# A sparse graph layer on one core: the last neighbour sums, the long rows and the search for uncovered rows in a new order

## The reference

```python
mask = A != 0
rank = jnp.cumsum(mask, axis=1) - 1
num_nbr = mask.sum(axis=1)
skip = jnp.where(num_nbr > 5, ceil(num_nbr / 2), 1)
keep = mask & ~((rank + 1) % skip[:, None] == 0)
n_keep = keep.sum(axis=1)
svals = jnp.sort(jnp.where(keep[:, :, None], x[None], big), axis=1)
agg = sum(1/3 * svals[row, max(ceil(q * n_keep) - 1, 0)] for q in (0.25, 0.5, 0.75))
agg = 0.5 * where(n_keep > 0, agg, 0) + 0.5 * x
out = agg @ W.T + b + x
```

## Time and profile before

| | |
|---|---|
| median of 3 runs | 160.31 us (160.06 to 160.69) |
| profiled execution, own time | 158.96 us |
| its span, first to last instruction | 157.1 us |
| busy, share of the span | DVE 66%, ACT 70%, PE 63%, POOL 46% |
| chain that ended last | DMA 53%, DVE 22%, PE 8%, issue 6%, POOL 6% |
| mean granted TensorE clock | 0.88 of full |

### The profile page before, as it was taken

One profiled execution on the slowest core, in us unless ns is written; L12 is line 12 of the kernel. 1 busy time (PEld: TensorE's weight loads), 2 busy tenths in 40 slices (PEclk: granted clock), 3 DMA queues, 4 the chain that ended last, 5 costly groups with the idle time before them and its releaser, 6 DMA issues.

```text
span 157.1 us, 2137 instructions
## 1 busy us (share of the span) xinstructions
PE 98.5 (63%) x568; PEld 52.3 (33%) x569; DVE 103.5 (66%) x449; ACT 110.0 (70%) x136; POOL 72.1 (46%) x118
## 2 busy tenths in 40 slices
PE   0009772778159763287765639854457979789892
PEld 0003321334023331123322114422123867658471
DVE  1002268425880649899972789889599989999931
ACT  3099999888888777887977898667779826363020
POOL 6898000000067772277770037776775068731030
PEclk9999999569965999758998555899977999999999
DMA  5999999999999999999999999999981043422002
GB/s 151 426 434 422 430 434 430 430 427 421 417 422 415 409 396 410 416 422 407 394 402 404 427 430 420 406 405 398 397 335 49 0 124 87 121 55 76 0 4 71
DMA packets 9571, 49.99 MB, mean 318 GB/s; under 512 B 1715, under 2 KB 5307, under 8 KB 6230
## 3 DMA queue, kind: packets, MB, share of 16 engines
q1 hardware_dynamic: 7648, 47.71, 74.8%
q0 software_dynamic: 1760, 2.07, 4.4%
q10 hardware_dynamic: 150, 0.07, 0.2%
HBM read 49.61 MB, written 1.71 MB: 327 GB/s over the span
## 4 chain that ended last, share of the span: by engine, by line
DMA 53%; DVE 22%; PE 8%; issue 6%; POOL 6%; ACT 2%; SPq 1%; POOLq 0%; DVEq 0%
DMA adj<-in_adj 49%; POOL gath_b L464 5%; PE ps_w L663 4%; DMA gath_b<-in_table,idx_b 4%; ACT sq L519 2%; DVE quads_a L1340 2%; DVE hot L911 2%; DVE rec L922 1%; DVE quads_b L1030 1%; DVE quads_b L1028 1%; PE ps_out L768 1%; POOL gath_a L464 1%; DVE merged L1028 1%; DVE merged L1030 1%; PE ps_out L775 1%
## 5 line engine op out<-in xcount | busy, mean ns | idle before, releaser
L519 ACT ACTIVATE sq<-adj 128x3328 bf16<-128x3328 int32 x26 | 77.4, 2977 | 21.9 <-DMA adj<-in_adj 21.9
L663 PE MATMUL ps_w<-sq,hot 128*128 128x416 bf16 x208 | 55.4, 420 | 23.0 <-DVE hot L911 23.0
L663 PEld LDWEIGHTS ps_w<-sq,hot 128*128 128x128 bf16 x208 | 19.4, 112 | 46.1 <-DVE hot L911 29.2
L464 POOL DMA_INDIRECT gath_a<-in_table,idx_a x12 | 12.5, 1044 | 48.5 <-DVEq L987 45.7
L464 POOL DMA_INDIRECT gath_b<-in_table,idx_b x24 | 25.4, 1060 | 7.3 <-issue 7.3
L911 DVE SCALAR_TENSOR_TENSOR hot<-slot_code,ps_place,strip_unit 128x256 bf16<-128x256 f32 (+1 forms) x22 | 11.1, 540 | 20.6 <-PE ps_place L641 19.6
L464 POOL DMA_INDIRECT gath_s<-in_table,idx_s x16 | 17.6, 1101 | 11.2 <-DVE idx_s L975 7.0
L911 DVE SCALAR_TENSOR_TENSOR hot<-slot_code,ps_out,strip_unit 128x256 bf16<-128x256 f32 (+1 forms) x22 | 11.1, 538 | 16.9 <-PE ps_out L641 15.2
L634 PE MATMUL ps_place<-level,mpart 64*128 64x2 bf16 x13 | 2.3, 176 | 19.8 <-ACT classes L529 19.8
L922 DVE MAX8 rec<-ps_w 128x8 f32<-128x208 f32 x32 | 9.7, 367 | 0.0
L634 PEld LDWEIGHTS ps_place<-level,mpart 64*128 64x128 bf16 x13 | 1.2, 96 | 24.9 <-issue 14.8
(11 more groups left out here) (276 smaller groups left out, 194.7 us busy)
## 6 DMA issues: line engine op xcount, KB each, us to landing
adj<-in_adj SPq DMA_DIRECT2D x26, 1664.0 KB, 12.6
out<-res SPq DMA_DIRECT2D x6, 192.0 KB, 2.2
xT<-in_xT SPq DMA_DIRECT2D x1, 896.0 KB, 17.8
xT<-in_xT SPq DMA_DIRECT2D x1, 768.0 KB, 15.7
gath_b<-in_table,idx_b POOLq DMA_INDIRECT x24, 6.2
gath_s<-in_table,idx_s POOLq DMA_INDIRECT x16, 4.7
out<-res SPq DMA_DIRECT2D x1, 256.0 KB, 2.3
out<-res SPq DMA_DIRECT2D x2, 128.0 KB, 1.9
```

The costliest lines, as they stand in the source:

```text
L464: nc.gpsimd.indirect_dma_start(slots[:, k, :], None, x_table, bass.IndirectOffsetOnAxis(ap=indices[:, k:k + 1], axis=0), bounds_check=TABL ...
L519: nc.scalar.activation(sq_ring[t % RING][:], adj_ring[t % RING][:], ACT.Square, accum_out=meta[:, t, 0:1]).then_inc(s_sq, 1)
L663: last = nc.tensor.matmul(ps_w[b % 2][h][:, 0:HW], hot[t % 3][:, s, :], sq_ring[t % RING][:, first:first + HW], start=False, stop=end and ...
```

## The change

Five edits, made together:

- The count of uncovered rows moves on VectorE from ahead of block 7's sort to behind `pick_last`; its sum on TensorE moves from ahead of `own_part_last` to behind `listed_part_last`; its cast moves behind the last copy; SP and GpSimd load it after their last transfers.
- The copy of `places` out of PSUM and the two instructions that make `mrec` and `mwords` move from VectorE to ScalarE.
- Block 6's picks are summed on TensorE, by three multiplications of 512 columns each (`turn_alone`); VectorE's two additions for it go. Block 7 gets these two additions instead (in `pick_last`) and is then turned like the other blocks, in two halves, so that `turn_last` with `ident`, `weigh_last` and one ScalarE copy go; VectorE copies the second half.
- The factors of the long rows are made on 16 partitions (`mweigh`), in five columns, spread by one multiplication, and used straight from PSUM.
- The transposes of `mgath` come ahead of `own_part_last`, the two `long_part`s ahead of `turn_last`, and `WARM` goes from 24 to 12.

```diff
@@ SyncE, GpSimd
-            sp.wait_ge(s_sln, 1)
-            n_slow = sp.value_load(slow_n[0:1, 0:1], min_val=0, max_val=N)
             for h in range(2):
...
+            sp.wait_ge(s_sln, 1)
+            n_slow = sp.value_load(slow_n[0:1, 0:1], min_val=0, max_val=N)
...
+            for k in range(2):
+                nc.gpsimd.memset(medge[:, k:k + 1], 15.0 - 2 * k)
+            for k in range(3):
+                nc.gpsimd.memset(msign[:, k:k + 1], 1.0 if k == 1 else -1.0)
@@ ScalarE
             find_spots(6)
+            act.wait_ge(s_hot, NT)
+            for k in range(2):
+                last = nc.scalar.activation(places[:, k:NT:2, :], ps_class[k], ACT.Copy)
+            last.then_inc(s_kept, 1)
             comb_copy(1)
             out_copy(0)
             out_copy(1)
+            act.wait_ge(s_mrec, 1)
+            nc.scalar.activation(mrec[:], ps_mrec, ACT.Copy)
+            nc.scalar.activation(mwords[:], ps_mrec[:, 3:35], ACT.Copy, scale=UNIT).then_inc(s_mcopy, 1)
...
             act.wait_ge(s_combps, NB)
-            nc.scalar.activation(comb[LAST % 2][:, 0:P], ps_comb[:, 0:P], ACT.Copy).then_inc(s_comb, 1)
-            act.wait_ge(s_yps, 1)
-            nc.scalar.activation(y_sb[:], ps_y, ACT.Copy).then_inc(s_y, 1)
+            nc.scalar.activation(comb[LAST % 2][:, 0:2 * P], ps_comb[:, 0:2 * P], ACT.Copy).then_inc(s_comb, 1)
@@ TensorE
+            def turn_alone():
+                pe.wait_ge(s_spots_late, ALONE - 1)
+                pe.wait_ge(s_comb, ALONE)
                 for k, part in enumerate((order[:, 1, :], pick[:, 0, :], pick[:, 1, :])):
                     pe.wait_ge(s_picks, k + 1)
-                    last = nc.tensor.matmul(ps_comb[:, 0:P], part, ident[:], start=(k == 0), stop=(k == 2))
+                    last = nc.tensor.matmul(ps_comb[:], part, late_at(ALONE), start=(k == 0), stop=(k == 2))
                 last.then_inc(s_combps, 1)
-            def weigh_last():
-                pe.wait_ge(s_comb, NB)
-                nc.tensor.matmul(ps_y, comb[LAST % 2][:, 0:P], w_pool[:], start=True, stop=True).then_inc(s_yps, 1)
+            def turn_last():
+                pe.wait_ge(s_spots_late, LAST - 1)
+                pe.wait_ge(s_comb, LAST)
+                pe.wait_ge(s_agg_s, 1)
+                for h, bank in enumerate((ps_comb, ps_w[1][0])):
+                    nc.tensor.matmul(bank[:, 0:2 * P], agg[:, LAST, :], late_spots[:, 3, 2 * h * P:(2 * h + 2) * P],
+                                     start=True, stop=True).then_inc(s_combps, 1)
...
             own_part(6)
+            turn_alone()
             pe.wait_ge(s_mdiag, 1)
-            nc.tensor.matmul(ps_mn, ones_f[0:MID, :], mdiag[:].rearrange("p a m -> p (a m)"), start=True,
-                             stop=True).then_inc(s_mwide, 1)
-            turn(6)
+            nc.tensor.matmul(ps_w[0][1][:, 256:256 + 5 * MID], ones_f[0:MID, :],
+                             mdiag[:].rearrange("p q m -> p (q m)"), start=True, stop=True).then_inc(s_mwide, 1)
             listed_part(6)
-            pe.wait_ge(s_slsum, 1)
-            nc.tensor.matmul(ps_slow, ones_f[:], slow_sum[:], start=True, stop=False)
-            nc.tensor.matmul(ps_slow, ones_f[0:MID, :], mbad[:], start=False, stop=True).then_inc(s_slps, 1)
-            own_part_last()
             pe.wait_ge(s_mgath, 32)
             for u in range(2):
                 last = nc.tensor.transpose(ps_mT[:, u * P:(u + 1) * P], mgath[:, u, :], ident[:])
             last.then_inc(s_mT, 1)
+            own_part_last()
             keep_busy(WARM)
             pe.wait_ge(s_magg, 1)
             nc.tensor.matmul(ps_my, maggT[:], wT[:], start=True, stop=True).then_inc(s_myps, 1)
             keep_busy(WARM_LATE)
+            for h in range(2):
+                long_part(h)
             turn_last()
-            long_part(0)
-            weigh_last()
-            long_part(1)
             listed_part_last()
+            pe.wait_ge(s_slsum, 1)
+            nc.tensor.matmul(ps_slow, ones_f[:], slow_sum[:], start=True, stop=False)
+            nc.tensor.matmul(ps_slow, ones_f[0:MID, :], mbad[:], start=False, stop=True).then_inc(s_slps, 1)
@@ VectorE, pick_last
+                dve.wait_ge(s_combps, ALONE + 1)
...
+                step(v.tensor_tensor(pick[:, 2, :], pick[:, 0, :], T[:, 1, :], ALU.add))
+                v.tensor_tensor(agg[:, LAST, :], pick[:, 2, :], pick[:, 1, :], ALU.add).then_inc(s_agg_s, 1)
+            def copy_comb_half():
+                dve.wait_ge(s_combps, NB + 1)
+                v.tensor_copy(comb[LAST % 2][:, 2 * P:4 * P], ps_w[1][0][:, 0:2 * P]).then_inc(s_comb_late, 1)
@@ VectorE, the factors of the long rows
-            v.tensor_scalar(mdiag[:, 0, :], ident[0:MID, 0:MID], n, None, ALU.mult)
...
-            step(v.tensor_scalar(mdiag[:, 1, :], ident[0:MID, 0:MID], mvalid[:, 1:2], None, ALU.mult))
-            dve.sem_inc(s_mdiag, 1)
+            v.tensor_tensor(mdiag[:], ident[0:MID, 0:MID].unsqueeze(1).broadcast_to([MID, 5, MID]),
+                            mweigh[:, 0:5].unsqueeze(2).broadcast_to([MID, 5, MID]), ALU.mult).then_inc(s_mdiag, 1)
...
+            dve.wait_ge(s_mwide, 1)
+            v.tensor_tensor(mpart[:, :, 0:4].rearrange("p m (s c) -> p s m c", c=2), msort[:, :, :, 4:6],
+                            ps_mn[:, 0:4, :].rearrange("p (s c) m -> p s m c", c=2), ALU.mult)
+            did(v.tensor_tensor(mpart[:, :, 4], msort[:, 1, :, 7], ps_mn[:, 4, :], ALU.mult))
```

More of the change, by code:

```diff
@@ L48 @@
 UNIT = float(1 << ID_BITS)
-WARM = 24
+WARM = 12
 WARM_LATE = 3
@@ L187, in build @@
         mkeys = sb("mkeys", [MID, MID], F32)
-        mdiag = sb("mdiag", [MID, 2, MID], F32)
+        mweigh = sb("mweigh", [MID, 7], F32)
+        mdiag = sb("mdiag", [MID, 5, MID], F32)
         msel = sb("msel", [P, 2, 8], F32)
@@ L500, in _ @@
                 bounds_check=ROWS - 1, oob_is_err=True, compute_op=ALU.add).then_inc(s_scat, 16)
+            pool.wait_ge(s_sln, 1)
+            n_slow = pool.value_load(slow_n[0:1, 0:1], min_val=0, max_val=N)
             with pool.If(n_slow > 0):
@@ L1168, in _ @@
                     merge_quads()
-            for k in range(2):
-                last = v.tensor_copy(places[:, k:NT:2, :], ps_class[k])
-            last.then_inc(s_kept, 1)
             merge_middle()
@@ L1190, in _ @@
             did(v.tensor_tensor(pb[:, :, 0, :], pg[:, :, 0, :], pg[:, :, 1, :], ALU.min))
-            dve.wait_ge(s_mrec, 1)
-            step(v.tensor_copy(mrec[:], ps_mrec))
-            whole = did(v.tensor_scalar(mwords[:], mrec[:, 3:35], UNIT, None, ALU.mult))
+            dve.wait_ge(s_mcopy, 1)
             g1 = did(v.tensor_scalar(mgone[:, 0:1], n, 12.0, 5.0, ALU.is_ge, ALU.add))
@@ L1284, in _ @@
                                          own_slot[:].unsqueeze(1).broadcast_to([P, 2, 8]), ALU.mult))
-            need(summed)
-            v.tensor_tensor(agg[:, ALONE, :], pick[:, 2, :], T[:, 1, :], ALU.add).then_inc(s_agg_s, 1)
             need(chosen)
@@ L1290, in _ @@
             v.tensor_copy(midx[:], midx_f[:]).then_inc(s_midx, 1)
+            dve.wait_ge(s_gath_s[1], KEYS * 16)
+            pg = gath_s[1][:].rearrange("p (a c) d -> p a c d", c=2)
+            low_high(pb[:, :, 0, :], pb[:, :, 1, :], pg[:, :, 0, :], pg[:, :, 1, :])
+            layer_done()
+            low_high(qa[:, :, 0, :], qa[:, :, 1, :], qb[:, :, 0, :], qb[:, :, 1, :])
+            layer_done()
+            low_high(B[:, :, 1, :], B[:, :, 2, :], A[:, :, 1, :], A[:, :, 2, :])
+            layer_done()
+            low_high(S[:, 3:11:7, :], S[:, 1:9:7, :], B[:, 0, 1:3, :], B[:, 1, 1:3, :])
+            low_high(S[:, 11, :], None, A[:, 0, 3, :], A[:, 1, 3, :])
+            low_high(None, S[:, 0, :], A[:, 0, 0, :], A[:, 1, 0, :])
+            layer_done()
+            low_high(S[:, 4:6, :], S[:, 6:8, :], S[:, 10:12, :], S[:, 0:2, :])
+            layer_done()
+            dve.wait_ge(s_mval, 1)
+            for m in range(MID):
+                for sign in range(2):
+                    last = v.max(msort[:, sign, m, :], mval[:, sign, m, :])
+            did(last)
+            layer_done()
+            dve.wait_ge(s_mwide, 1)
+            v.tensor_tensor(mpart[:, :, 0:4].rearrange("p m (s c) -> p s m c", c=2), msort[:, :, :, 4:6],
+                            ps_mn[:, 0:4, :].rearrange("p (s c) m -> p s m c", c=2), ALU.mult)
+            did(v.tensor_tensor(mpart[:, :, 4], msort[:, 1, :, 7], ps_mn[:, 4, :], ALU.mult))
+            layer_done()
+            v.tensor_reduce(maggT[:], mpart[:], AX.X, ALU.add).then_inc(s_magg, 1)
+            pick_last()
+            dve.wait_ge(s_kept, 1)
             counts = rec[:, :, 0]
@@ L1322, in _ @@
-            layer_done()
-            low_high(B[:, :, 1, :], B[:, :, 2, :], A[:, :, 1, :], A[:, :, 2, :])
-            for q, (edge, op) in enumerate(((13.0, ALU.is_ge), (13.0, ALU.is_lt), (15.0, ALU.is_lt), (15.0, ALU.is_ge))):
-                last = v.scalar_tensor_tensor(out=mwt[:, q, :], in0=ps_mn[:, 0:MID], scalar=edge,
```

(22 more changed lines are left out.)

88 lines of the change are left out of this document (35 added, 53 removed).

## The result

| | before | after |
|---|---|---|
| median of 11 runs each, same chip | 160.31 us (159.43 to 160.69) | 162.38 us (160.93 to 164.07) |
| profiled execution, own time | 158.96 us | 161.56 us |
| its span | 157.1 us | 159.8 us |

The ratio is 1.0131, 95% interval 1.0101 to 1.0162: the changed kernel is slower, where 159.0 and faster had been forecast. Read by the stages of the forecast, the way to the last copy did become shorter, and the end took back more than all of it. A ratio here leaves out executions that ran more than 1.5% above the fastest of their kernel, while a median counts them all, so the two need not agree.

A forecast was written before the change was run, and what follows sets the result against it. Bound: adjacency loads until the last tile, then VectorE until `maggT`, then handovers between TensorE, ScalarE and VectorE. Gains 0.82 + 0.23 + 0.42 = 1.47 less a 0.2 loss at the end: 160.31 - 1.27 = 159.04 us, range 158.2 to 160.2.

The forecast's parts named there:

- the stages of the forecast: How much earlier three places come: first MAX8 0.82 us, `maggT` 1.05, last copy 1.47.
- The end: After the last copy: SyncE's late load of the count makes 2.1 us against 1.9, a loss of 0.2.
- the sign: Listed as showing the forecast wrong: more than 3 us from the last write's issue to the span's end.
- the count shows at the end: Rival, chance 0.12: four engines' loads, branches and closing barrier in a row behind the last sum, 0.9 more, 159.9 us.
- The first MAX8: Block 7's sort: starts 0.82 us earlier, set by `mval` over `turn_alone` (2.75); VectorE idle 1.0 before sort, 0.6 before MAX8.
- Weights and the tail: Weighing to reduction 0.34 us instead of 0.57, gain 0.23; from `maggT` to the last copy gain 0.42, bounds 0.1 to 0.6.
- The count had its margin: Between `agg` and VectorE's last copy: the count (0.91 us) has a margin of 0.35 and costs nothing.
- Costed at nothing: Early part: `s_kept` from ScalarE starts `own_part(1)` about 0.5 us later, covered by TensorE's 0.93 idle before `hot_mid`.
- The clock rival: Rival, chance 0.05: fewer dummies let TensorE's clock fall to half from `maggT` on, 3 us more, 162.0 us.
- the side that I had forecast: Whole kernel: faster, chance 0.66, against same 0.27 and slower 0.07.

The follow-up runs named there:

- the kernel with `turn(6)`: Changed kernel with the count of uncovered rows moved back early, block 6 back to one turn and its two additions on VectorE: 159.80 us, ratio 0.9870.
- the version with the early count and no drain: Changed kernel with the count of uncovered rows and its loads moved back early, GpSimd's closing drain left out: 158.59 us, ratio 0.9856.

## Why the prediction was wrong

**The step that failed is "The end".** It held that "the last write's landing, 1.9 after its issue, was all that SyncE waited for", and followed SyncE alone: a loss of 0.2. SyncE's side came out a little better: it is done 155.89 - 153.64 = 2.25 behind the last copy, 2.27 before. The load took 0.47 instead of 0.76, and it lies beside the landing. What was left out is that the span ends with the last of all engines, and that the same edit delays GpSimd, whose closing drain had run beside the write's landing, until 4.57 behind the addition, and, at 156.9 against SyncE's 156.75, had even ended last by 0.16. Moving its release from 151.2 to 155.0 moves the end. The drain is in the trace of before, at the line of the block's end. A sequencer instruction is neither busy time nor a row of the timeline, but by line it shows. I had the row of 5695 ns before the forecast and did not use it. The term was 0.2 and measured 3.5. That is shown three ways: by taking away what releases the drain late, by taking away the drain, and by making the late count alone. The prediction had named the sign: more than 3 us from the last write's issue to the span's end. The issue ended at 153.16 + 0.89 = 154.05, the span at 159.81.

The 0.2 had one part that the prediction compared with the Trainium skill, the 0.45 from SyncE's branch to its next instruction. It is 0.5 in the trace after too (154.9 to 155.4), but no run here shows that it is a fetch of instructions.

**The rival "the count shows at the end"** had the place right, with "the loads of four engines, their branches and the closing barrier" in a row, but priced it with 0.9; the row that gave the price of the barrier on GpSimd was not used. A chain of loads was not it: with three engines' loads still late the end was 2.89.

**The first MAX8:** 0.88 earlier, forecast 0.82. The way there was as described but for its parts. `turn_alone` took 2.74 (2.75):

```profile
139.50 1.02 PE L765 MATMUL ps_comb<-adj,order 128*128 128x512 f32 x2
...
140.36 1.88 PE L765 MATMUL ps_comb<-adj,pick 128*128 128x512 f32 x4
...
142.28 0.60 ACT L546 ACTIVATE comb<-ps_comb 128x512 f32<-128x512 f32 x1 [1.84 <-PE ps_comb L765]
...
144.61 0.78 ACT L623 ACTIVATE adj<-ps_w 128x128 f32<-128x128 f32 x4
```

VectorE waited 1.20 ahead of the sort (1.0) but only 0.16 ahead of the MAX8 (0.6). The gather of block 7, issued at 136.93, let the sort start 3.0 later, not 2.3 to 2.6, and in the changed kernel without a drain the wait was 2.04. There the first MAX8 came 0.73 later than in the trace after, and 0.15 earlier than in before. Why the gather lands late in some executions stays open. The forecast of 0.82 had the right chain in the trace after, ScalarE's; it had no term for such a gather.

**Weights and the tail.** The reduction starts 0.35 behind the first weighing instruction (0.34 forecast, 0.57 before). From `maggT` on the gain was 0.24 and not 0.42, inside the bound of 0.1 to 0.6. Counted from `maggT`, `agg` was ready 0.07 later than summed, the first half's turn ended 0.14 later, and the last copy 0.17 later. The count had its margin: VectorE is through with it at 151.62 and waits 0.38 for the second half (0.35).

**Costed at nothing, and nothing:** `s_kept` on ScalarE makes `own_part(1)` wait 0.55, and `collect_mid` still waits 0.28 for `hot_mid`; from block 7's words to `hot_mid` it is 4.50 before and 4.49 after.

**The clock rival** did not come: 1.00 in every stretch from 138 to 154. But such a fall does happen: the kernel with `turn(6)` shows it, behind an idle stretch of 1.35 us, and the trace with six dummies in that stretch does not. The long `turn_alone` had kept TensorE busy there. That this was part of its worth is likely, not shown, and no term of my sum held it. The Trainium skill, "TensorE: Matmul & The Clock Gate", Part 1, says that idle time brings the lower clock and sustained work the higher. The trace with the fall agrees: 0.50 behind the idle stretch, 1.00 again from 152 on, behind work without a break. The trace with the dummies has an idle stretch of 1.45 us without a fall.

Without the closing drain the changed kernel ran in 157.87, ratio 0.9862, which is the side that I had forecast; it and the version with the early count and no drain (0.9856) are the best of this study. By the stages, the change is worth 1.35 us on the way of its own trace, and the end 0.13 (2.66 less 2.53), 1.5 in all. The ratio says 2.2 us, but its interval reaches from 1.4 to 3.0, so the two do not contradict each other. In both SyncE itself still waits until the addition and all writes have landed. The ordinary closing can be kept at no cost in the trace (2.45 against 2.46 to 2.53) by draining early.

## What to carry to other kernels

The end of a kernel is the latest of all its engines, not that of the engine that waits for the last write. Before an instruction is moved behind the last transfer, list what each engine has still to do after it, with the sequencer's instructions and the closing barrier, and read their durations by line. If GpSimd has issued indirect gathers, let it drain in an idle stretch, or release it early. And where work is taken from TensorE, ask what keeps its clock up in its place.

## What the runs showed of the hardware

- GpSimd's drain takes 4.47 to 4.64 us when it first follows this kernel's 54 indirect gathers, however long the engine has been idle since (1.3 to 3.8 us in these traces); 0.04 us ahead of them; 0.12 when a drain has been taken behind them and the addition is 2.8 us past. Right behind the addition it ends 1.4 to 1.5 us after it, if the gathers have been drained. How the 4.5 us grow with the number of gathers was not tried.
- An idle stretch of 1.35 us (0.65 of 2 us busy) was followed by a fall of the granted clock from 1.00 to 0.50, where it stayed from 144 to 150 with TensorE busy all through; in the changed kernel it was 1.00 over the same stretch. In another trace an idle stretch of 1.45 us (0.55 of 2 us busy) was not followed by a fall.
